# Cross-attention on one core: the order in which TensorE takes values, scores and maxima within a step

## The reference

```python
x = (hidden_states - mu) * jax.lax.rsqrt(var + LN_EPS) * ln_gamma + ln_beta
Q = _split_heads(x @ Wq.T)            # 2 x 32 heads x 512 x 32
K = _split_heads(memory_keys)         # 2 x 32 heads x 1024 x 32; V the same rows
scores = jnp.einsum('bhsd,bhtd->bhst', Q, K) * scale
scores = jnp.where(mask, scores, -jnp.inf)
probs = jax.nn.softmax(scores, axis=-1)
attn = jnp.einsum('bhst,bhtd->bhsd', probs, V)
out = attn.reshape(B, S, HIDDEN) @ Wout.T
return residual + out
```

## Time and profile before

| | us |
|---|---|
| median of three runs | 727.6 (726.88 to 728.45) |
| the profiled execution, own time | 726.73 |
| its span | 724.9 |
| TensorE matmuls busy | 679.5 (94%) |
| VectorE busy | 460.0 (63%) |
| GpSimd busy | 391.8 (54%) |
| ScalarE busy | 339.2 (47%) |
| mean granted TensorE clock | 0.976 |

### The profile page before, as it was taken

One profiled execution on the slowest core, in us unless ns is written; L12 is line 12 of the kernel. 1 busy time (PEld: TensorE's weight loads), 2 busy tenths in 40 slices (PEclk: granted clock), 3 DMA queues, 4 the chain that ended last, 5 costly groups with the idle time before them and its releaser, 6 DMA issues.

```text
span 724.9 us, 10759 instructions
## 1 busy us (share of the span) xinstructions
PE 679.5 (94%) x3537; PEld 398.5 (55%) x3537; DVE 460.0 (63%) x494; ACT 339.2 (47%) x614; POOL 391.8 (54%) x107
## 2 busy tenths in 40 slices
PE   2789999865999999999999999999999999899998
PEld 2568788633454544444545444444444445578886
DVE  6763333049787786877878868778687676543231
ACT  3741211433566656566666566665666566500000
POOL 1000000045397977968879779797797897910000
PEclk9799999977999999999999999999999999999999
DMA  9621000425245253351542624525335203123231
GB/s 351 175 50 53 30 29 1 109 62 130 56 108 127 64 131 85 79 144 47 129 104 60 156 50 112 127 63 130 78 84 124 67 1 118 58 88 117 86 116 58
DMA packets 40287, 68.10 MB, mean 94 GB/s; under 512 B 5669, under 2 KB 22695, under 8 KB 40239
## 3 DMA queue, kind: packets, MB, share of 16 engines
q1 hardware_dynamic: 40212, 67.64, 34.2%
q10 hardware_dynamic: 36, 0.01, 0.0%
HBM read 25.18 MB, written 4.19 MB: 41 GB/s over the span
## 4 chain that ended last, share of the span: by engine, by line
PE 87%; DVE 4%; ACT 3%; SPq 2%; DMA 2%; issue 2%; POOL 0%; ACTq 0%; DVEq 0%; POOLq 0%
PE MX L910 20%; PE PV L950 17%; PE SX L934 17%; PE MX L1064 12%; PE MX L940 5%; PE PV L873 5%; PE SX L873 5%; PE MX L850 2%; PE MX L920 1%; ACT PR L606 1%; PE SX L865 1%; DMA PR<-in_x 1%; ACT PR L523 1%; DVE QT L723 1%; PE MX L844 1%
## 5 line engine op out<-in xcount | busy, mean ns | idle before, releaser
L728 DVE TENSOR_REDUCE mx<-MX 128x1 f32<-128x1024 f32 x256 | 302.3, 1217 | 114.3 <-PE MX L910 109.7
L606 ACT ACTIVATE PR<-SX 128x512 f32<-128x512 f32 x512 | 268.9, 601 | 179.3 <-PE SX L934 173.7
L484 POOL TENSOR_TENSOR acc<-acc,PR 128x2048 f32<-128x2048 f32 x64 | 293.4, 4585 | 18.1 <-ACT PR L606 12.7
L484 POOL TENSOR_TENSOR acc<-PR 128x2048 f32<-128x2048 f32 x16 | 73.3, 4584 | 226.4 <-ACT PR L606 226.4
L910 PE MATMUL MX<-R 97*128 97x512 f32 x512 | 176.5, 428 | 18.2 <-DVE mx L728 8.4
L934 PE MATMUL SX<-R 99*128 99x512 f32 x512 | 175.8, 420 | 3.7 <-ACT PR L606 3.3
L910 PEld LDWEIGHTS MX<-R 97*128 97x128 f32 x512 | 86.0, 191 | 114.6 <-DVE mx L728 89.2
L950 PE MATMUL PV<-PR,C 128*32 128x512 f32 x1024 | 137.8, 611 | 0.1
L934 PEld LDWEIGHTS SX<-R 99*128 99x128 f32 x512 | 94.5, 191 | 65.7 <-ACT PR L606 36.5
L819 DVE TENSOR_TENSOR PR<-PR,MX 128x512 f32<-128x512 f32 x16 | 10.9, 687 | 53.3 <-PE MX L1064 51.8
L1064 PE MATMUL MX<-R 128*128 128x512 f32 x192 | 44.3, 390 | 0.0
(11 more groups left out here) (82 smaller groups left out, 487.1 us busy)
## 6 DMA issues: line engine op xcount, KB each, us to landing
R<-KTh SPq DMA_DIRECT2D x64, 256.0 KB, 4.3
PR<-in_x SPq DMA_DIRECT2D x16, 512.0 KB, 4.2
C<-in_ctx SPq DMA_DIRECT2D x16, 512.0 KB, 3.4
R<-KTl SPq DMA_DIRECT2D x64, 128.0 KB, 3.9
R<-QT SPq DMA_DIRECT2D x64, 128.0 KB, 2.5
acc<-in_L_xattn_Wq SPq DMA_DIRECT2D x8, 512.0 KB, 3.7
R<-QT SPq DMA_DIRECT2D x64, 64.0 KB, 2.1
C<-in_L_xattn_Wout SPq DMA_DIRECT2D x8, 512.0 KB, 3.3
```

The costliest lines, as they stand in the source:

```text
L484: nc.gpsimd.tensor_tensor(acc[:, :, :], a, PR[:, tt % RING, :, :], ALU.add).then_inc(pool_used, 1)
L606: nc.scalar.activation(PR[:, tt % RING, h, :], SX[(HPG * tt + h) % BANKS][:, :], ACT.Exp, scale=SCALE).then_inc(exp_done, 1)
L728: nc.vector.tensor_reduce(mx[:, u % 2, i:i + 1], MX[par][:, :], mybir.AxisListType.X, ALU.max, negate=True).then_inc(mx_freed, 1)
```

## The change

`values` of tile 0 stays behind the scores 0 and 1 of tile 1, and `values` of tile 7 behind those of the next step's tile 0. The values of tiles 1 to 6 are now taken two tiles at a time, in one block behind the scores and items of tiles 3, 5 and 7. The table has a fourth list, `behind`, for items that follow such a block. In `STEP` there is now one maximum behind each pair of scores and one behind the blocks of tiles 3 and 5; the item `bias` goes behind `maxima(2, 0)` and the scores 2 and 3 of tile 6. `FIRST_STEP` is laid out in a similar way. ScalarE and VectorE follow the same table.

```diff
 STEP = [
-    ([], maxima(1, 4), keys(2)),
-    ([], sums(-1), maxima(1, 5)),
-    ([], maxima(1, 6), maxima(1, 7)),
-    (maxima(1, 8), maxima(1, 9), maxima(1, 10)),
-    ([], maxima(1, 11), maxima(1, 12)),
-    (maxima(1, 13), maxima(1, 14), maxima(1, 15)),
-    ([], bias(1) + maxima(2, 0), maxima(2, 1)),
-    ([], maxima(2, 2), maxima(2, 3)),
+    ([], maxima(1, 4), keys(2), []),
+    ([], sums(-1), maxima(1, 5), []),
+    ([], maxima(1, 6), maxima(1, 7), []),
+    ([], maxima(1, 8), maxima(1, 9), maxima(1, 10)),
+    ([], maxima(1, 11), maxima(1, 12), []),
+    ([], maxima(1, 13), maxima(1, 14), maxima(1, 15)),
+    ([], maxima(2, 0), bias(1) + maxima(2, 1), []),
+    ([], maxima(2, 2), maxima(2, 3), []),
 ]
...
-                for tt, (early, with_01, with_23) in enumerate(items):
+                for tt, (early, with_01, with_23, behind) in enumerate(items):
                     score(n, u, tt, 0)
                     score(n, u, tt, 1)
                     for item in early:
                         mx_item(*item)
-                    if tt >= 1:
-                        values(n, u, tt - 1)
-                    elif not first:
+                    if tt == 1:
+                        values(n, u, 0)
+                    elif tt == 0 and not first:
                         values(n - 1, u + RING - 1, TT - 1)
                     for item in with_01:
                         mx_item(*item)
                     score(n, u, tt, 2)
                     score(n, u, tt, 3)
                     for item in with_23:
+                        mx_item(*item)
+                    if tt >= 3 and tt % 2:
+                        values(n, u, tt - 2)
+                        values(n, u, tt - 1)
+                    for item in behind:
                         mx_item(*item)
```

More of the change, by code:

```diff
@@ L95 @@
 FIRST_STEP = [
[L96 to L101, removed]
-    (maxima(1, 13), maxima(1, 14), maxima(1, 15)),
-    ([], bias(1) + maxima(2, 0), maxima(2, 1, 2, 3)),
+    ([], [], [], []),
+    ([], maxima(1, 0), maxima(1, 1), []),
+    (maxima(1, 2), maxima(1, 3), keys(2), []),
+    (maxima(1, 4), maxima(1, 5), maxima(1, 6), maxima(1, 7)),
+    ([], maxima(1, 8), maxima(1, 9), []),
+    ([], maxima(1, 10), maxima(1, 11), maxima(1, 12)),
+    ([], maxima(1, 13), maxima(1, 14, 15), []),
+    ([], bias(1) + maxima(2, 0), maxima(2, 1, 2, 3), []),
 ]
 STEP = [
-    ([], maxima(1, 4), keys(2)),
-    ([], sums(-1), maxima(1, 5)),
-    ([], maxima(1, 6), maxima(1, 7)),
-    (maxima(1, 8), maxima(1, 9), maxima(1, 10)),
-    ([], maxima(1, 11), maxima(1, 12)),
-    (maxima(1, 13), maxima(1, 14), maxima(1, 15)),
-    ([], bias(1) + maxima(2, 0), maxima(2, 1)),
-    ([], maxima(2, 2), maxima(2, 3)),
+    ([], maxima(1, 4), keys(2), []),
[6 more added lines that the diff above has]
+    ([], maxima(2, 2), maxima(2, 3), []),
 ]
@@ L125, in items_of @@
     if n == STEPS - 2:
-        items[TT - 1] = ([], wout(0), wout(1))
+        items[TT - 1] = ([], wout(0), wout(1), [])
     if n == STEPS - 1:
-        items = [([], [], []) for _ in range(TT)]
+        items = [([], [], [], []) for _ in range(TT)]
         for o, tt in zip(range(2, WOUT_BLOCKS), (1, 2, 3, 5, 6, 7)):
-            items[tt] = ([], sums(-1) if tt == 1 else [], wout(o))
+            items[tt] = ([], sums(-1) if tt == 1 else [], wout(o), [])
     return items
@@ L634, in step @@
                     exp(n, tt, 3)
-                    at = high_and_bias(n, with_23, at)
+                    at = high_and_bias(n, with_23 + behind, at)
                     if isinstance(n, int) and n == STEPS - 1 and tt == TT // 2:
```

## The result

| | kernel before | changed kernel |
|---|---|---|
| median | 727.8 (726.9 to 728.5, 4 runs) | 742.6 (742.1 to 743.6, 4 runs) |
| ratio | | 1.0203, 95% interval 1.0188 to 1.0218 |
| span of the profiled execution | 724.9 | 740.3 |
| TensorE matmuls busy | 679.5 | 673.2 |
| VectorE maxima busy; idle before them | 302.3; 114.3 | 298.9; 142.0 |

The account below looks back on a forecast made before the run. TensorE sets the pace, but joined blocks make it wait for VectorE's two MX banks: +12.1 - 0.3 + 0.8 + 1.5 = +14.1 on 726.7, 740.8; median 0.9 above, 741.7 us, range 736 to 748 (chance 0.81).

Parts of the forecast that it names:

- the saving on TensorE: Each of three joins a step saves 0.42 us, 1.26 in all; with 0.3 at the step boundary, 1.5.
- the boundary wait and the loop jump: At the step start: the first score's 0.42 idle and ScalarE's jump to its loop head would be hidden.
- The walk of one step: One loop step traced from its first score pair through VectorE's two MX banks: 30.33 us against 29.31.
- signs named ahead: In the trace: ticks about 30.3, blocks of 1.85, waits 0.8 ahead of pair 13 and 0.9 ahead of pair 21.
- The transpose: VectorE's 0.70 us L750 behind maximum 10 adds 0.65; maximum 11 starts at 17.66 and pair 13 waits for it.
- the new place of the bias: In tile 6: pair 21 lands in 20's bank, at 25.77, one whole maximum that nothing can run under.
- 13 ticks, from the first to the fourteenth sums: Loop steps of 30.33 us instead of 29.31: 394.3 - 382.2 = +12.1, error -4 to +5.
- step 0, from its first pair on: First step: keys come 1.9 us earlier, then 20 maxima on VectorE set the end: -0.3, between -2 and +1.
- step 14: Same run from maximum 5 to 15 as in the loop, no later maxima: +0.8 us, between 0 and 1.5.
- step 15 to the last sums: Values 3 and 4 move behind the gap, 2.14 us later less one join: +1.5, between 0 and 3.
- Rival 1: In the loop: VectorE keeps up, 27.8 us a step, -22 over 13 steps, about 703 in all; chance 0.08.
- Rival 2: In the loop: bias rows arrive late; 1 us late is +13, 755; chance 0.05 with other added waits, above 748.

Follow-up runs that it names:

- experiments 1 and 2: Each VectorE maximum covers only half of its columns: 1, in the changed kernel, 710.8 us; 2, in the kernel before, 720.3 us.
- experiments 3 and 4: 3: changed kernel, VectorE's 0.70 us transpose moved behind tile 7's items, 736.6 us. 4: kernel before, bias moved behind maximum 0 and scores 2 and 3, 738.9 us.
- experiment 5: Changed kernel with the bias back ahead of maximum 0 of the step after next: 750.1 us, ratio 1.0307.
- Experiment 7: Kernel before with the values of tile 6, still a single block, behind tile 7's last item instead of in its middle: 729.9 us.

## Why the prediction was right

**The views and the saving on TensorE.** The join saves what the rows said: 1.85 for 16 matmuls, and the boundary wait and the loop jump go. As a saving it is real (experiments 1 and 2), though 0.92 a step there, not 1.5, with the bias in its new place.

**The walk of one step.** Predicted and measured, from the first scores (342.95, one tick ahead of 373.11): pair 5 8.36 and 8.26; pair 9 12.58 and 12.48; maximum 10 on VectorE 15.87 and 15.76; 11 at 17.66 and 17.52; pair 14 20.07 and 19.90; pair 15 22.58 and 22.41; pair 21 25.77 and 25.59; next step 30.33 and 30.16. The mechanism and its places were right; of the 0.17 too much, 0.10 are there at pair 5, and the rest comes in steps of 0.01 to 0.04. Of the signs named ahead, TensorE's own rows show 0.80 idle ahead of pair 21 (0.9 was named) and 0.51 ahead of pair 13 (0.8 was named; 0.95 at its weight load).

**The transpose and the bias.** Shown by experiments 3 and 4: 0.61 a step for the one, and for the other 0.86 in the kernel before. The prediction speaks of the new place of the bias as a cost alone. Only experiment 5 showed that it is the better one once the blocks are joined.

**The sum.** The total fits better than its terms:

| term | predicted | measured |
|---|---|---|
| 13 ticks, from the first to the fourteenth sums | +12.1 | +9.6 (391.8 against 382.2) |
| step 0, from its first pair on | -0.3 | +3.4 (47.1 against 43.6) |
| start of that pair | 0 | -0.7 |
| step 14 | +0.8 | +0.5 |
| step 15 to the last sums | +1.5 | +2.5 |
| sum on the span | +14.1 | +15.4 |

(The prediction calls these sums the second to the fifteenth; the first ones, those of step 0, are in step 1 at 194.54, so it is the first to the fourteenth. The 382.18 is right.) The loop was 0.17 a tick too dear, and its last interval, which already holds step 14's part without keys, is 29.82.

The mis-sized term is step 0, outside the range given for it (-2 to +1). The sentence that failed is that keys come 1.9 earlier and the 20 maxima on VectorE set the end. The first part holds in direction: from the first pair to the pair behind the long wait it takes 18.4 (168.63) instead of 19.6 (170.49 in the kernel before), 1.2 less. But from there to the pair of the last maximum it takes 2.5 more, with the values of four tiles there as before: the first joined block runs at the lower clock, and the bias, with no block ahead of it any more, waits 1.06 for VectorE. And the maxima do not set the end. The values of tiles 1 and 2 used to be done ahead of the long wait; now those of tiles 5 and 6 are left over and stand behind the last maximum, where nothing hides them. The pair of that maximum and the first sums, in the changed kernel and then before:

```profile
189.58 0.74 PE L911 MATMUL MX<-R 97*128 97x512 f32 x2 [0.40 <-DVE mx L729]
...
197.13 1.90 PE L941 MATMUL MX<-PR,ones 128*32 128x512 f32 x16
```

```profile
188.89 0.73 PE L910 MATMUL MX<-R 97*128 97x512 f32 x2 [0.40 <-DVE mx L728]
...
194.35 1.90 PE L940 MATMUL MX<-PR,ones 128*32 128x512 f32 x16
```

That is 7.55 against 5.46, 2.1 more. Experiment 7 has the single block of tile 6 at this place and loses 2.0 in step 0, too. The errors of the loop and of step 0 have opposite signs, so the 0.9 us between forecast and result flatters the prediction: part of it is luck.

For step 15, +1.5 became +2.5, and all of it lies behind the gap in which a score waits for ScalarE (1.98; before: 1.68). From the score at its end to the last sums it takes 23.7 (634.36 to 658.02) against 21.2 (621.46 to 642.64). The joined block there takes 3.06 instead of 1.85 at a granted clock of 0.50, but the clock is 0.50 behind the gap in the kernel before as well (622 to 624, where eight transposes take 1.56 instead of 0.79), so this alone is no difference. What only the changed kernel has is that TensorE waits for ScalarE in the two tiles behind the block:

```profile
640.42 0.50 PE L935 MATMUL SX<-R 99*128 99x512 f32 x1 [0.30 <-ACT PR L607]
...
642.80 0.51 PE L935 MATMUL SX<-R 99*128 99x512 f32 x1 [0.30 <-ACT PR L607]
```

ScalarE had been idle for 4.00 ahead of these tiles. How the extra 1.0 divides between the two was not tested.

**The rivals.** Rival 1, VectorE keeps up, is excluded by the tick of 30.16; with maxima of 0.69 instead of 1.22 the kernel comes near its 27.8 (experiment 1: 27.98). Its price was 1.2 us too high for 27.8 a step: 13 x 27.8 is 20.8 under 382.2, not 22. Rival 2 did not happen: the first score shows no wait, and the first of the two bias transfers landed 1.8 after its issue in all 16 steps.

## What to carry to other kernels

In this kernel an engine that is idle a quarter of the time sets the pace, because the engine ahead of it offers work in bursts and there are only two buffers. So before joining instructions into longer blocks, walk one period with the pitch of the consumer and the number of buffers, and look at which item the item two places on must wait for. What seems lost between blocks may be what hides the other engine's time (experiment 7), so here the join paid only together with items moved into the consumer's idle stretch. And the place of a short item that takes a whole buffer can be worth about as much as the joins (0.86 a step against 0.92): its best place depends on what stands around it, so it is tried again after every other move. Last, steps outside the loop are walked by themselves: the largest error here was in one of them.

## What the runs showed of the hardware

The clock is not full everywhere in the written-out steps. In the changed kernel TensorE waits 8.11 in step 0 for VectorE, and behind it a joined block runs slowly; the order of time, and the stretches of the view by windows (stretch, length, then busy time of PE, PEld, DVE, ACT, POOL, the granted clock, and DMA):

```profile
168.63 1.22 PE L911 MATMUL MX<-R 97*128 97x512 f32 x2 [8.11 <-DVE mx L729]
169.78 3.64 PE L951 MATMUL PV<-PR,C 128*32 128x512 f32 x16
173.36 1.18 PE L911 MATMUL MX<-R 97*128 97x512 f32 x2
```

```profile
162.00:174.00 12.00, 5.37 (x20) 1.65 (x21) 8.90 (x5) 0.00 (x0) 4.82 (x2) 0.50 0.73 181
174.00:180.00 6.00, 6.00 (x30) 3.28 (x32) 5.42 (x5) 4.19 (x8) 2.90 (x1) 0.97 0.00 0
```

The granted clock is 0.50 from the wait until about 174, the lower of the two levels (1.2 GHz), and the 16 matmuls take 3.58 instead of 1.85. The kernel before has the same behind its wait of 7.47 (0.64 in 170 to 176; its pairs are 0.85 apart there instead of 0.47), so only what stands in this stretch has changed: the values of two tiles where there had been scores, maxima and the values of one. The start of step 0's first pair, which waits for a transfer, lies between 150.25 and 152.77 in the eleven profiles of these kernels, though nothing ahead of it was edited; two single profiles can differ by 2.5 us for that alone, which is why the steps were compared by ticks.
